# Second layer's experts: up-products with the weights stationary, down-products in float16 parts, and a new split of the weights

## What is computed

```python
def _L1_ffn_ref(hidden_states, gate_w, sgate_w, w13, w2, shared_gate_up_w, shared_down_w):
    x = hidden_states.reshape(-1, H)                 # 2048 x 256 (the kernel's x)
    shared = _silu_and_mul(x @ shared_gate_up_w.T) @ shared_down_w.T       # 704 wide
    shared = shared * jax.nn.sigmoid(x @ sgate_w.T)
    routing_weights = jax.nn.softmax((x @ gate_w.T).astype(jnp.float32), axis=-1)   # 16 experts
    topk_w, topk_ids = jax.lax.top_k(routing_weights, 4)
    def body(acc, ew):
        w13_e, w2_e, e = ew
        coef = jnp.sum(jnp.where(topk_ids == e, topk_w, 0.0), axis=-1)
        h = _silu_and_mul(x @ w13_e.T)               # gate and up, 176 wide each
        return acc + (h @ w2_e.T) * coef[:, None], None
    sparse_out, _ = jax.lax.scan(body, init, (w13, w2, jnp.arange(16)))
    return (shared + sparse_out).reshape(B, S, H)
```

## Time and profile before

| | |
|---|---|
| median of 3 runs | 1427.73 us (1426.43 to 1430.14) |
| profiled execution | 1428.56 us, span 1426.4 us |
| busy share of the span | PE 83%, PEld 52%, DVE 63%, ACT 46%, POOL 42% |
| batch 0 of the shared expert, 1058.4 to 1095.9 | 37.5 us |
| routed loop, 1095.9 to 1304.2 | 208.3 us, PE at work in 206.1 |
| batches 1 to 3 and sums, 1304.2 to 1426.4 | 122.3 us, PE at work in 94.3 |

### The profile page before, as it was taken

How to read it: one execution, slowest core, us unless ns; L and a number is a source line. 1 busy time by engine, 2 the same in 40 slices (tenths; PEclk the granted TensorE clock), 3 DMA queues, 4 the chain that set the end, 5 groups by cost and what they waited for, 6 DMA issues and landing times.

```text
span 1426.4 us, 23057 instructions
## 1 busy us (share of the span) xinstructions
PE 1177.9 (83%) x6337; PEld 745.1 (52%) x6338; DVE 898.5 (63%) x2098; ACT 652.2 (46%) x1687; POOL 605.4 (42%) x629
## 2 busy tenths in 40 slices
PE   5837178781679899899889889899987999999786
PEld 3425144330356566666666656666654666664443
DVE  4866804586487777878866787776645444443545
ACT  2413023352565576576566555666644444442111
POOL 0378944451143334443333344344431444442744
PEclk9959589896799999999999999999998999999898
DMA  8176019986321111213101000002036333332422
GB/s 277 37 274 263 15 36 255 331 297 241 118 84 65 63 53 63 72 48 113 36 12 50 30 30 31 30 30 91 1 107 185 103 103 103 103 101 68 126 78 82
DMA packets 92214, 149.98 MB, mean 105 GB/s; under 512 B 11296, under 2 KB 64160, under 8 KB 89312
## 3 DMA queue, kind: packets, MB, share of 16 engines
q1 hardware_dynamic: 82144, 120.60, 25.5%
q0 software_dynamic: 9984, 28.32, 6.9%
HBM read 103.74 MB, written 45.15 MB: 104 GB/s over the span
## 4 chain that ended last, share of the span: by engine, by line
PE 44%; DVE 13%; issue 10%; POOL 8%; ACT 7%; DMA 6%; DVEq 4%; POOLq 4%; ACTq 2%; SPq 2%
PE ps L985 6%; PE ps L1057 6%; PE ps L1169 5%; PE ps L1016 4%; PE ps L1181 4%; ACT arena L1411 3%; PE ps L1179 2%; POOL wvo L2240 2%; POOLq L2156 2%; DMA arena<-in_wdn 2%; DVEq L1833 2%; PE ps L1000 2%; ACTq L1413 2%; PE ps L1124 2%; POOL arena L2154 2%
## 5 line engine op out<-in xcount | busy, mean ns | idle before, releaser
L2201 POOL TENSOR_TENSOR arena<-arena 128x512 f32<-128x512 f32 x128 | 161.5, 1273 | 345.4 <-ACT arena L1388 344.7
L985 PE MATMUL ps<-arena 128*128 128x512 f16 x768 | 179.9, 385 | 0.0
L2206 POOL TENSOR_TENSOR arena<-arena 128x768 f32<-128x768 f32 x64 | 104.8, 1638 | 106.1 <-DVE arena L1838 106.1
L1387 ACT ACTIVATE arena<-ps 64x512 f32<-64x512 f32 x128 | 76.1, 595 | 142.6 <-DVE arena L1810 139.1
L1411 ACT ACTIVATE arena<-arena 128x192 f32<-128x192 f32 x256 | 113.0, 444 | 13.2 <-DVEq L1833 12.5
L985 PEld LDWEIGHTS ps<-arena 128*128 128x128 f16 x768 | 76.1, 99 | 79.4 <-issue 4.7
L1816 DVE TENSOR_TENSOR arena<-arena 128x512 f32<-128x512 f32 x128 | 108.3, 885 | 7.2 <-POOL arena L2201 6.7
L1042 PE MATMUL ps<-arena 128*128 128x192 f32 (+1 forms) x512 | 91.0, 320 | 22.3 <-ACT arena L1393 21.9
L1810 DVE TENSOR_TENSOR arena<-ps,arena 128x512 f32<-128x512 f32 x128 | 85.3, 686 | 36.0 <-PE ps L985 35.3
L1042 PEld LDWEIGHTS ps<-arena 128*128 128x128 f32 x512 | 85.7, 192 | 38.5 <-issue 31.1
L1057 PE MATMUL ps<-wvo,arena 128*128 128x256 f16 x768 | 94.0, 282 | 12.5 <-ACT arena L1397 7.2
(11 more groups left out here) (280 smaller groups left out, 2386.5 us busy)
## 6 DMA issues: line engine op xcount, KB each, us to landing
z_d<-wvo SPq DMA_DIRECT2D x4, 4096.0 KB, 28.2
arena<-z_d SPq DMA_DIRECT2D x16, 1024.0 KB, 5.9
arena<-wqk_d SPq DMA_DIRECT2D x16, 1024.0 KB, 5.0
arena<-in_wgu SPq DMA_DIRECT2D x32, 384.0 KB, 8.9
y_d<-wvo SPq DMA_DIRECT2D x80, 128.0 KB, 1.9
arena<-in_wdn SPq DMA_DIRECT2D x32, 192.0 KB, 11.3
arena<-in_w13T SPq DMA_DIRECT2D x4, 1408.0 KB, 13.3
wqk_d<-arena SPq DMA_DIRECT2D x4, 1024.0 KB, 4.1
```

The costliest lines, as they stand in the source:

```text
L985: last = pe.matmul(ps[s][:, :], wqk[gg][:, s * DC + c, w, hh * DH:(hh + 1) * DH], hx[bb][:, :, x, c * P:(c + 1) * P], start=(c == 0 and w ...
L2201: nc.gpsimd.tensor_tensor(qk_s[:, s], qk_s[:, s], sin, ALU.mult).then_inc(sin_done, 1)
L2206: nc.gpsimd.tensor_tensor(a, a, ri.unsqueeze(2).to_broadcast([P, TPB, KW]), ALU.mult).then_inc(pn_done, 1)
```

## The change

- `up_proj`: the weights are stationary and the 128 rows' columns move. The 352 weight columns are laid in another order, and three groups (112 gate, 112 up, 64 up + 64 gate columns) are made one after the other, each with two halves and three parts: 18 matmuls. h comes out turned, so `turn_h` and its evacuation go. `h1` is [112 or 64, 2 x 128] per tile, gate by two activations, product by two DVE instructions.
- h gets a high part (ACT) and a low part (DVE); `down_proj` is six float16 matmuls, with 112 and 64 rows.
- w2a is split by ACT and DVE, w2b by POOL (eight rounds of scale, copy, subtract) between the barrier and its first gather; PE waits for both.
- The shared expert's down-products become float16 too: hs and sdw get parts; `shared_product` writes in place. All splits are numbered in one order, `PART`, and wait in that order.
- Rows of odd and even tiles use two PSUM banks. The waits for the clearing of z_d move to SP.

```diff
-        SPLIT_AFTER = [range(0), range(0), range(0), range(0, 2), range(2, 4), range(4, E1)]
+        SPLIT_AFTER = [[("sd", 0), ("sd", 1)], [("sd", 2), ("sd", 3)], [("sd", 4), ("sd", 5)],
+                       [("w13", e) for e in range(0, 2)], [("w13", e) for e in range(2, 4)],
+                       [("w13", e) for e in range(4, E1)] + [("w2", g) for g in range(E1 // 2)]]
...
             sp.wait_ge(share_ready, 1)
-            sp.dma_start(xn_d.rearrange("(n p) e -> p n e", p=P)[:, :, D:D + E0], exA0).then_inc(share_kept, 16)
-            sp.wait_ge(share_kept, 16)
+            sp.dma_start(xn_d.rearrange("(n p) e -> p n e", p=P)[:, :, D:D + E0], exA0).then_inc(z_clear, 16)
+            sp.wait_ge(z_clear, 16 * 5)
...
-                    last = pe.matmul(ps[4 + k][:, 0:D], hsT[0:rows, c, k * P:(k + 1) * P], sdw[0:rows, c], start=(c == 0), stop=(c == FC - 1))
+                    for x, w in PARTS:
+                        last = pe.matmul(ps[4 + k][:, 0:D], hs16[0:rows, c, x, k * P:(k + 1) * P], sdw16[0:rows, c, w],
+                                         start=(c == 0 and x == w), stop=(c == FC - 1 and x == 1))
...
-            pe.wait_ge(w2_in, 32)
-            pe.wait_ge(lo_done, 4 * UNITS + SGU + E1)
+            pe.wait_ge(lo_done, parts_of("w2", E1 // 2 - 1))
+            pe.wait_ge(w2b_ready, 1)
...
-            def up_proj(e, lhs, bank):
-                for c in range(DC):
-                    for x, w in PARTS:
-                        last = pe.matmul(ps[bank][:, 0:2 * F1], lhs[:, x, c * P:(c + 1) * P],
-                                         w13[:, bass.ds(e, 1), w, c * 2 * F1:(c + 1) * 2 * F1].rearrange("p a f -> p (a f)"),
-                                         start=(c == 0 and x == w), stop=(c == DC - 1 and x == 1))
+            def up_proj(e, rows, bank):
+
+                for to, (at, n) in enumerate(((0, F1A), (F1A, F1A), (2 * F1A, 2 * F1B))):
+                    for c in range(DC):
+                        for w, x in PARTS:
+                            first = c * 2 * F1 + at
+                            last = pe.matmul(ps[bank][0:n, to * P:(to + 1) * P],
+                                             w13[:, bass.ds(e, 1), w, first:first + n].rearrange("p a f -> p (a f)"),
+                                             rows[:, x, c * P:(c + 1) * P],
+                                             start=(c == 0 and x == w), stop=(c == DC - 1 and w == 1), skip_group_check=True)
+                return last
+
+            def down_proj(e, u, bank):
+
+                for rows, w2, at in ((slice(0, F1A), w2a16, 0), (slice(0, F1B), w2b16, P)):
                     for x, w in PARTS:
+                        last = pe.matmul(ps[bank][:, 0:D], h16[rows, u, x, at:at + P], w2[rows, bass.ds(e, 1), w].rearrange("p a d -> p (a d)"),
+                                         start=(at == 0 and x == w), stop=(at == P and x == 1))
                 return last
...
-                upto(pe, h1_ready, j)
-                upto(pe, h1T_rd, j - 1)
-                turn_h(k % 2).then_inc(h1T_ps, 1)
...
-                upto(pe, h1T_rd, j)
+                upto(pe, h1_lo, j)
                 upto(pe, y1_rd, j - 2)
...
+            def gate_out(j, u):
+                upto(act, gu1_ps, j)
+                upto(act, h1_lo, j - 2)
+                nc.scalar.activation(h1[0:F1A, u % 2, 0:P], ps[1 + u][0:F1A, 0:P], ACT.Silu, scale=DOWN)
+                nc.scalar.activation(h1[0:F1B, u % 2, P:2 * P], ps[1 + u][F1B:2 * F1B, 2 * P:3 * P], ACT.Silu, scale=DOWN).then_inc(sg1_ready, 1)
+
+            def h_high(j, u):
+                upto(act, h1_ready, j)
+                upto(act, y1_ps, j - 2)
+                nc.scalar.activation(h16[:, u, 0], h1[:, u], ACT.Copy, scale=UP_H).then_inc(h1_hi, 1)
...
+            def shared_rest(b, c):
+                rows = min(P, FS - c * P)
+                dve.wait_ge(hi_done, parts_of("hs", b, c))
+                nc.vector.scalar_tensor_tensor(hs16[0:rows, c, 1], sgs[0:rows, c % 2], UP_H, hs16[0:rows, c, 0], ALU.mult, ALU.subtract)\
+                    .then_inc(lo_done, 1)
...
+            pool.wait_ge(w2_in, 32)
+            rows = slice(0, F1B)
+            for e in range(0, E1, 2):
+                rest(pool, "pool")
+                nc.gpsimd.tensor_scalar(w2b[rows, e:e + 2], w2b[rows, e:e + 2], UP_W, None, ALU.mult)
+                pool.drain()
+                rest(pool, "pool")
+                nc.gpsimd.tensor_copy(w2b16[rows, e:e + 2, 0], w2b[rows, e:e + 2])
+                pool.drain()
+                rest(pool, "pool")
+                nc.gpsimd.tensor_tensor(w2b16[rows, e:e + 2, 1], w2b[rows, e:e + 2], w2b16[rows, e:e + 2, 0], ALU.subtract)
+                pool.drain()
+            pool.sem_inc(w2b_ready, 1)
```

More of the change, by code:

```diff
@@ L510, in build @@
         w13_raw = R7.take(P, E1, DC, 2 * F1)
-        w2a = R7.take(P, E1, D)
-        R7.at = max(R7.at, R6_gap)
+        hs16 = R7.take(P, FC, 2, SEQ, dt=F16)
+        assert R7.at <= R6_gap
+        R7.at = R6_gap
         SGU = 2 * DC
@@ L519, in build @@
         sgw = R7.take(P, SGU, FS)
+        sdw16 = R7.take(P, FC, 2, D, dt=F16)
+        R7.at -= (FC - 1) * D
         sdw = R7.take(P, FC, D)
@@ L525, in build @@
         assert R7.at <= R6_tail
-        hsT = R7.take(P, FC, SEQ)
-        w2b = R7.take(F1 - P, E1, D)
+        w2a16 = R7.take(P, E1, 2, D, dt=F16)
+        R7.at -= (E1 - 2) * D
+        w2a = R7.take(P, E1, D)
+        w2b16 = R7.take(P, E1, 2, D, dt=F16)
+        R7.at -= (E1 - 2) * D
+        w2b = R7.take(P, E1, D)
         sgs = R7.take(P, 2, SEQ)
-        sg1 = R7.take(P, 2, F1)
         wv_flat, wo_flat = wvo[:, 0:UNITS * 512], wvo[:, UNITS * 512:(2 * UNITS + 1) * 512]
@@ L1474, in shared_gate, with shared_high @@
                 upto(act, gus_ps, n)
-                upto(act, hs_ready, n - 2)
+                if n >= 2:
+                    act.wait_ge(lo_done, parts_of("hs", (n - 2) // FC, (n - 2) % FC))
                 nc.scalar.activation(sgs[0:rows, c % 2], ps[2 * (c % 2)][0:rows, :], ACT.Silu, scale=DOWN).then_inc(sgs_ready, 1)
+            def shared_high(b, c):
+                n, rows = FC * b + c, min(P, FS - c * P)
+                upto(act, hs_ready, n)
+                if c == 0 and b:
+                    upto(act, ys_ps, TPB * b - 1)
+                nc.scalar.activation(hs16[0:rows, c, 0], sgs[0:rows, c % 2], ACT.Copy, scale=UP_H).then_inc(hi_done, 1)
@@ new lines, in weight_high @@
+            def weight_high(kind, k):
+                if kind == "sd":
+                    if k == 0:
+                        act.wait_ge(ffn_in, 48)
+                    if k >= 1:
+                        act.wait_ge(lo_done, parts_of("sd", k - 1))
+                    rows = min(P, FS - k * P)
+                    high = nc.scalar.activation(sdw16[0:rows, k, 0], sdw[0:rows, k], ACT.Copy, scale=UP_W)
+                elif kind == "w13":
+                    if k == 0:
+                        act.wait_ge(ffn_in, 48 + 16 * DC)
+                    if k == E1 // 2:
+                        act.wait_ge(w13_in, 16 * DC)
+                    if k >= 2:
+                        act.wait_ge(lo_done, parts_of("w13", k - 2))
+                    high = nc.scalar.activation(w13[:, k, 0], flat(w13_raw[:, k]), ACT.Copy, scale=UP_W)
+                else:
+                    if k == 0:
+                        act.wait_ge(w2_in, 32)
+                    if k >= 1:
+                        act.wait_ge(lo_done, parts_of("w2", k - 1))
+                    high = nc.scalar.activation(w2a16[0:F1A, 2 * k:2 * k + 2, 0], w2a[0:F1A, 2 * k:2 * k + 2], ACT.Copy, scale=UP_W)
+                high.then_inc(hi_done, 1)
@@ L1490, in rows_out @@
+                if c == FC - 1:
+                    shared_high(0, c)
+                for part in SPLIT_AFTER[c]:
+                    weight_high(*part)
             def rows_out(j, u):
@@ L1512, in routed @@
                 if not (last_tiles and k >= 2):
-                    gate_out(gu1_ps, h1_ready, sg1_ready, j + 2, (k + 2) % 4)
+                    gate_out(j + 2, (k + 2) % 4)
+                if not (last_tiles and k >= 3):
+                    h_high(j + 1, (k + 1) % 2)
             for j in range(3):
@@ L1947, in tables @@
                     nc.vector.tensor_reduce(zA, exA, AX.X, ALU.add)
-                    nc.vector.tensor_scalar(sgA, sgA, 1.0, None, ALU.add)
+                    nc.vector.tensor_scalar(sgA, sgA, 1.0, UP_H * UP_W, ALU.add, ALU.mult)
+                    dve.drain()
+                    nc.vector.tensor_scalar(zA, zA, UP_H * UP_W, None, ALU.mult)
                     dve.drain()
@@ L2044, in routed @@
                 if not (last_tiles and k >= 2):
-                    product(sg1_ready, h1T_ps, h1_ready, j + 2, (k + 2) % 4)
+                    product(j + 2, (k + 2) % 4)
+                if not (last_tiles and k >= 3):
+                    h_low(j + 1, (k + 1) % 2)
                 upto(dve, y1_ps, j)
@@ L2052, in _ @@
             for j in range(2):
```

(4 more changed lines are left out.)

127 lines of the change are left out of this document (70 added, 57 removed).

## The result

| | before | after |
|---|---|---|
| median | 1427.49 us (1426.43 to 1430.14, 4 runs) | 1512.56 us (1506.59 to 1513.73, 4 runs) |
| profiled execution, span | 1428.56, 1426.4 | 1506.59, 1504.8 |
| ahead of the feed-forward part | 1058.4 | 1050.7 |
| front: batch 0 of the shared expert and the splits, to the first up-product | 37.5 | 72.3 |
| loop of the routed experts | 208.3 | 263.3 |

The account below looks back on a forecast made before the run. PE's array was taken to bound the routed loop, its sequencer second, 1.5 us under per four-tile turn. From 1428.6, +58 (sequencer), +32.6 (loop start) and -4.5 (shared experts) gave 1514.7, put at 1514 us; range 1450 to 1570.

Parts of the forecast that it names:

- step 2: PE's sequencer in the routed loop: ten more address computations a tile at 0.12 us, 3.26 us a tile, +58 us.
- B: Routed loop: address work doesn't grow or hides, array's 2.11 us sets the pace, 1423 us; faster below about 2.15; chance 0.18.
- rival C: Routed loop, in between: address steps of 0.07 us or slow loads at 2.6 to 2.8 a tile, 1462 to 1478; chance 0.15.
- step 1: PE's array in the routed loop: 2.11 us a tile, 0.43 under now, up to 2.8 with slower loads.
- step 3: Start of the routed loop: POOL's w2 rounds take 30 us ahead of its gathers, first up-product +32.6 us (+22 to +41).
- step 4: Shared experts, batches 1 to 3: shorter float16 down-products and DVE's 5.56 us wait moved to ACT, -4.5 us (-9 to +1).
- step 5: Clearing waits moved to SP before the end of stage 2, and two multiplications in tables: nothing.
- Rival D: Jump back of PE's longer loop turn fetches code, 2.8 us each 19 times, +53 on A (1514), 1567; chance 0.12.

Follow-up runs that it names:

- experiment 2: Changed kernel with each tile's expert weights fixed, so no weight address is computed and two of four expert-number reads go: ratio 0.9996, loop 173.5 us.
- experiment 5: Changed kernel with the first four tiles' gathers moved first and POOL's eight rounds left out, second down-product reading w2a's rows: ratio 1.0313, front 49.0 us.
- the repeat: Changed kernel run again unaltered: ratio 1.0582, front 73.1, loop 263.1, tail 119.2 us.
- experiment 6: Changed kernel with DVE's wait for the third product of the block before put back ahead of each shared product: ratio 1.0624, tail 119.2 us.
- the kernel with 88 + 88 rows: Kernel before with the 176 rows of h and w2 cut into 88 + 88 instead of 128 and 48: ratio 0.9915, loop 189.1 us.
- experiment 8: Kernel before with 96 + 80 rows, plus PE's w2 wait moved behind two tiles' up-products: 0.9854; w2 on ACT's queue instead: 0.9923; both: 0.9911.

## Why the prediction was right, point by point

**The sequencer (step 2), +58 us.** Right in mechanism and size. 16 computations a tile, 12 and 4, are in the trace; each costs 0.124 us (forecast 0.12); a turn takes 13.02 us (13.0), a tile 3.26 (3.26), the loop grew by 55.0. About 1 of the missing 3 us is that I set 3.26 against the ordinary tile of 2.54, and not against the mean of 2.56. The two tests that bear on it went opposite ways: no address and fewer reads of the expert, -90 us; 12 addresses in the kernel before, +42. Rivals B and C fall as descriptions of this kernel; B is what experiment 2 measured. Its point of decision held too: with 2.14 us a tile the kernel came out level with before (0.9996).

**The array (step 1), 2.11 us a tile.** Hidden in the changed kernel, laid open by experiment 2: 2.14. The up-products were 1.00 (0.99); down-products 0.76 and row turns 0.37 to 0.39 where I had 0.65, 0.22 and 0.25 of switching, 1.12 in all: the same sum. The upper end of 2.8 and rival C's slow loads fall. The Trainium skill (TensorE: Matmul & The Clock Gate, Weight-path perf modes) has loads of fewer than 128 columns go the slow way, which would have made it 0.093 us for each of 112 columns, an estimate; the trace of experiment 2 doesn't agree, its 112-column matmuls stood 0.055 apart.

**The start of the loop (step 3), +32.6 us.** Measured +34.8. POOL's rounds were 30 us in the sum and took 31.4, but the parts of a round weren't right: the scaling took 1.5 to 1.7 where I had 1.0, the copy 0.60 where I had 1.0, the subtraction 1.15 to 1.5. w2 landed 31.3 us after the stage's begin, 32.1 before. The 14 us, less the gathers' head start, that I gave to ACT and DVE without POOL were 11.5 in experiment 5. What I had wrong is the share of the gathers: they can be moved for 3.5 us, not for their own length, since PE's wait stands ahead of the row turns.

**The shared experts (step 4), -4.5 us.** Measured -3.7, -3.0 in the repeat, from the shorter down-products that the step also names, 3.2 us in batch 2 and 3.0 in batch 3, less what is lost around them. The reason given, DVE's wait of 5.56 us, was wrong: without it DVE waits for ACT instead, and experiment 6 puts it back at no cost. The step itself said that "that wait goes to ACT", and counted the gain all the same.

**z_clear and the tables (step 5), nothing.** No run shows more: the stages ahead of the feed-forward part vary by 16 us between executions of the changed kernel's family, so a small effect there can't be seen in one trace, and the medians leave -1 us for it.

**Rival D, code fetched at each jump back.** It didn't come. It would have added 2.8 us to each of 19 turns. A turn takes 13.02 us where the sum without a fetch has 13.0, and the sequencer's branch at 1205.2 is followed at 1205.6 by the read of the next expert's number. The longest tile of a turn is 0.8 us over the shortest, and experiment 2, with the same jump, has 2.15 us beside 2.13. The Trainium skill (Runtime: NRT & Kernel Launch, Instruction fetch mechanics) speaks of a stall when a jump leaves the window of two blocks of code. A turn that went from some 170 to 300 instructions shows none here.

**The sum.** 1514 against 1512.56. The terms' errors were -3, +2.2 and +0.8 us, small each; that they cancel to nothing is luck, and so in part is the size of step 4, one of whose two reasons was wrong.

## What to carry over

Where a loop picks its weights by a register, count the addresses per turn beside the matmuls: turning an operand around can leave the array's work as it is and multiply the addresses, and no busy share shows them. A wait costs from the place where it stands in its engine's program, not from where its data is used; put it in front of the first reader. A wait that ends a standstill also costs what the lower clock behind it makes of the next work. Before rewriting a stage for an idle load between two tile sizes, try another cut of the rows: here that alone was worth 19 us of loop. And don't take a loop's pace from its ordinary tile: add up a whole turn, with the tile in which it jumps back.

## What the runs showed of the hardware that I had not expected

- A register-dependent weight address costs PE 0.124 us once PE's sequencer is the bound, from 14 to 16 of them a tile as between two neighbours in the trace; the six of the kernel with 88 + 88 rows were hidden under 2.20 us of matmuls, but for the tile of each turn with the branch, 2.64 us.
- Loads of 112 float16 columns kept up with matmuls of 128 columns, 0.055 us apart.
- w2 moved into 88 partitions at 157 GB/s on the mean over 19.5 us (the start of a 0.5 MB transfer behind it included), into 96 and 80 at 201 (likewise), into 112 at 250 and 64 at 185, into 128 at about 350, all with rows of 1 KB from the same tensor.
- After PE had stood still for 6.33 us its granted clock was 0.50 and twelve up-products took 3.70 us; where it had stood still for at most 1.4 us the clock was 1.00 and they took 2.33 (experiment 8).
- Two queues with w13 and w2 at once moved about 300 GB/s together, where w13 alone in one queue had 390 to 400 for most of its time.
